# Softmax in a fused gated cross-attention and expert layer: the exponential per group of 64 columns, from PSUM, with its sums

## The chip, the cores and the metric

The kernel runs on one core of one Trainium2 chip. The metric is device time in microseconds (us) of one execution. Engines: PE (TensorE, matmuls), DVE (VectorE), ACT (ScalarE), POOL (GpSimd), SP (issues DMAs). The engines run their own instruction streams in order and wait for one another through semaphores.

## The reference, cut to what matters

1024 tokens (16 sequences of 64) of width 256 go through a layer norm, self attention and cross attention with quantised projections, a gated residual, and a mixture of 16 experts with top-2 routing. The part that the change touches is the softmax of both attentions:

```python
def _gqa(q, k, v):
    scale = 1.0 / np.sqrt(q.shape[-1])
    scores = jnp.einsum('bsghd,btgd->bghst', q, k) * scale
    p = jax.nn.softmax(scores, axis=-1)
    return jnp.einsum('bghst,btgd->bsghd', p, v)
# 8 groups g, 2 heads h per group, head width 128, 64 queries s and 64 keys t for each sequence b
...
core = _gqa(q, k, v).reshape(b, s, nh * d)
...
xout = _gqa(qx, kx, vx).reshape(b, s, nh * d)
```

## The kernel before

The tokens are cut into 8 tiles of 128 (two sequences each). A tile t takes one pass of four steps c = 0 to 3; step number n = 4t + c. Steps c = 0, 1 are self attention, c = 2, 3 cross attention, each for half of the heads. In one step PE makes four projections of 512 columns (`project`, i = 0 to 3: keys, two banks of queries, values), and the work is a pipeline over steps: step n projects for n, transposes the normalised heads of n-1, computes and normalises the scores of n-2, transposes the probabilities and multiplies by the values for n-3, and projects the output of n-4. Tile 0 also carries the preparation of the weights ("folds"). Behind the 8 tiles comes the expert part, which the change does not touch.

The order on each engine is written out by hand in its function `step`; the passes t = 1 to 6 are a hardware loop, the others unrolled. In a step ACT does, in this order: `evacuate` 0 (L647, PSUM to SBUF), `prob_copy` (L692), `norm_bank0` (L668, four 128x128 scalings), `evacuate` 1, the exponential `expo` (L687), `evacuate` 2, `heads_out` 0 (L682), `values_out` (L655), `heads_out` 1 and 2, and `roots` (L659 logarithm, L661 exponential: the inverse square root of the head variance). POOL does the softmax division `normalise` (L535), then `variance` (L509, L511), `coefficients` (L517 to L523, from ACT's root to `cw`), then `norm_bank` 1 and 2 (L529); in step c = 2 also the rounding of the next tile's inputs (L501, L503). ACT's `norm_bank0` waits for `cw` (`coef_done`). DVE does `stats` 0 (L1243), `softmax_in` (L1251 maximum, L1254 subtraction), `stats` 1, `softmax_sum` (L1260, L1263), `stats` 2, and the scaling and quantisation of the attention output (L1270, L1203 to L1214).

The scores of a step stand in one PSUM bank, `score_ps`: 128 partitions (2 heads x 64 queries) by 8 groups of 64 keys. PE uses the same bank for `head_transposes` i = 1 and then for the next scores. PE's order in a step: projection 0, probability transposes, scores, projection 1, values, output, projection 2, head transposes 0, projection 3, head transposes 1 and 2. `ge(engine, semaphore, count)` is a wait that is left out where the count is not positive. `prob` and `probT`, `probn` and the like are parts of `reg1` and `reg2`, which the profile calls `reg`; `raw` is part of `rot`.

Of the kernel before, what the change touches and what calls it, by code (L numbers as in the profile page):

```python
# [24 lines left out]
F32 = mybir.dt.float32  # L25
# [4 lines left out]
ALU = mybir.AluOpType  # L30
ACT = mybir.ActivationFunctionType
AX = mybir.AxisListType
# [76 lines left out]
def build(nc, x, cols, rowc, ident, cen, tri, slot, ctxT, wkvN, wqN, wkN, wvN, wqxN, wpT, rwT, wffn, out):  # L109
    ctx = ExitStack()  # L110
    with ctx:
# [77 lines left out]
        mx = sb("mx", [P, 8], F32)  # L189
        sm = sb("sm", [P, 8], F32)  # L190
        rinv = sb("rinv", [P, 2, 8], F32)
# [152 lines left out]
        max_done = sem("max_done")  # L344
        sub_done = sem("sub_done")
        exp_done = sem("exp_done")
        sum_done = sem("sum_done")
        rinv_done = sem("rinv_done")
# [248 lines left out]
        def _(act):  # L597
# [87 lines left out]
            def expo(w, s):  # L685
                act.wait_ge(sub_done, w + 1)
                act.activation(prob[s], prob[s], ACT.Exp, scale=SCORE_SCALE).then_inc(exp_done, 1)  # L687

# [114 lines left out]
        def _(pe):  # L803
# [61 lines left out]
            def head_transposes(n, c, i):  # L865
                pe.wait_ge((norm0_done, norm1_done, norm2_done)[i], n + 1)
                if i == 1:
                    ge(pe, sub_done, n)
                else:
                    ge(pe, headT_evac, 3 * n + (0, 0, 1)[i])  # L870
# [10 lines left out]
            def scores(w, s):  # L881

                pe.wait_ge(headT_evac, 3 * w + 3)
                ge(pe, sub_done, w)
                for g in range(4):
                    for b in range(2):
                        mm = pe.matmul(score_ps[:, (2 * g + b) * S:(2 * g + b + 1) * S], qT[:, s, 2 * g + b, :],  # L887
                                       kT[:, s, g, b * S:(b + 1) * S], start=True, stop=True)
                mm.then_inc(score_done, 1)
# [229 lines left out]
        def _(ve):  # L1119
# [128 lines left out]
            def softmax_in(w, s):  # L1248
# [3 lines left out]
                ve.wait_ge(max_done, w + 1)  # L1252
                ge(ve, probn_done, w - 1)
                ve.tensor_tensor(prob[s].rearrange("p (g t) -> p g t", t=S), s3,  # L1254
                                 mx[:, :].unsqueeze(2).to_broadcast([P, 8, S]),
                                 ALU.subtract).then_inc(sub_done, 1)

            def softmax_sum(w, s):
                ve.wait_ge(exp_done, w + 1)
                ve.tensor_reduce(sm[:, :], prob[s].rearrange("p (g t) -> p g t", t=S), AX.X,  # L1260
                                 ALU.add).then_inc(sum_done, 1)
                ve.wait_ge(sum_done, w + 1)
                ve.reciprocal(rinv[:, s, :], sm[:, :]).then_inc(rinv_done, 1)  # L1263

# [280 lines left out]
```

## Time and profile before

| | |
|---|---|
| three runs | 478.61, 479.4, 489.06 us; median 479.4 |
| profiled execution | 479.9 us, of which the span from first to last instruction is 478.1 |
| PE busy | 416.2 us (87%) |
| DVE busy | 371.3 us (78%) |
| ACT busy | 281.3 us (59%) |
| POOL busy | 277.4 us (58%) |
| granted TensorE clock, mean | 0.96 of full |

The busy shares are means over a preparation, eight passes and the expert part, which have different limits. A row of the profile names line, engine, operation and tiles (out<-in); "idle" in a row is how long the engine stood still just before the instruction, and the name behind the arrow is what ended that wait.

### The profile page before, as it was taken

What the parts mean: (1) busy time and instruction counts of PE and PEld (TensorE: products, weight loads), DVE (VectorE), ACT (ScalarE), POOL (GpSimd) and SP (SyncE); (2) the same over time, 40 slices, a digit from 0 to 9 for tenths busy, and PEclk for the clock granted to TensorE, in tenths of its full rate; (3) what the DMA queues carried; (4) which work ended last, traced back from release to release, by engine and by line L of the source; (5) the groups of instructions that cost most, each with busy time, mean ns of one, the idle gap of its engine ahead of it and who ended that gap; (6) DMA issues with size and microseconds to landing.
All of it is one profiled execution on the core that took longest, in us unless ns stands there. A gap on an engine that the chain in (4) does not pass through costs nothing.

```text
span 478.1 us, 9942 instructions
## 1 busy us (share of the span) xinstructions
PE 416.2 (87%) x2982; PEld 312.6 (65%) x2982; DVE 371.3 (78%) x832; ACT 281.3 (59%) x610; POOL 277.4 (58%) x401
## 2 busy tenths in 40 slices
PE   0488899999999999999999999999897697999910
PEld 0446567767767776776776777677785585888710
DVE  5987798999999998899899999999679561323236
ACT  3689867767677767867776767777640322333310
POOL 2056496596686867669658677665420660366660
PEclk9989999999999999999999999999888799999975
DMA  8946719999600000000000000000680223244207
GB/s 211 272 156 79 99 60 313 287 318 276 174 0 0 0 0 0 0 0 0 0 0 0 0 0 0 0 3 2 247 346 1 77 101 99 83 123 130 91 19 254
DMA packets 34810, 45.66 MB, mean 95 GB/s; under 512 B 3034, under 2 KB 32223, under 8 KB 33888
## 3 DMA queue, kind: packets, MB, share of 16 engines
q1 hardware_dynamic: 26656, 35.61, 24.0%
q0 software_dynamic: 6992, 9.46, 9.0%
q10 hardware_dynamic: 1136, 0.27, 0.3%
q8 instruction: 13, 0.21, 0.2%
q14 instruction: 13, 0.11, 0.1%
HBM read 28.34 MB, written 24.32 MB: 110 GB/s over the span
## 4 chain that ended last, share of the span: by engine, by line
PE 42%; DVE 18%; POOL 15%; issue 11%; ACT 7%; DMA 5%; SPq 1%; POOLq 1%; ACTq 0%; DVEq 0%
PE proj_ps L860 9%; PE score_ps L887 7%; PE proj_ps L1017 6%; PE pv_ps L909 4%; PE out_ps L919 3%; POOL zbuf L570 3%; POOL xin L501 3%; POOL rot L529 3%; DVE st L1243 3%; DVE yv L1270 2%; ACT rot L647 2%; PE probT_ps L895 2%; PE headT_ps L878 2%; POOL reg L535 2%; ACT qT L682 2%
## 5 line engine op out<-in xcount | busy, mean ns | idle before, releaser
L860 PE MATMUL proj_ps<-arena 128*128 128x512 f16 x384 | 99.7, 382 | 3.9 <-POOL arena L503 3.9
L1243 DVE BATCH_NORM_STATS2 st<-rot 128x6 f32<-128x256 f32 x192 | 72.7, 420 | 13.9 <-ACT rot L647 12.8
L529 POOL TENSOR_TENSOR rot<-rot,cw 128x512 f32<-128x512 f32 x64 | 67.3, 1072 | 2.5
L647 ACT ACTIVATE rot<-proj_ps 128x512 f32<-128x512 f32 x96 | 56.4, 588 | 20.3 <-PE proj_ps L860 18.5
L535 POOL TENSOR_TENSOR reg<-reg,rinv 128x512 f32<-128x512 f32 x32 | 34.6, 1083 | 52.8 <-DVE rinv L1263 52.8
L887 PE MATMUL score_ps<-kT,qT 128*128 128x64 f32 x512 | 62.0, 275 | 0.6 <-ACT qT L682 0.5
L887 PEld LDWEIGHTS score_ps<-kT,qT 128*128 128x128 f32 x512 | 60.3, 193 | 2.4 <-ACT qT L682 2.2
L668 ACT ACTIVATE rot<-rot,cw 128x128 f32<-128x128 f32 x128 | 40.9, 390 | 30.2 <-POOL cw L523 30.2
L860 PEld LDWEIGHTS proj_ps<-arena 128*128 (+1 forms) x384 | 37.4, 103 | 29.6 <-issue 6.2
L852 PE MATMUL proj_ps<-arena 128*128 128x512 f16 x192 | 46.7, 379 | 0.0
L1435 DVE TENSOR_TENSOR arena<-proj_ps,arena 128x256 f32<-128x256 f32 x24 | 10.1, 422 | 46.4 <-ACT arena L754 46.4
L589 POOL DMA_INDIRECT ybuf<-arena,bslot x32 | 31.5, 983 | 24.7 <-DVE arena L1447 19.1
L1270 DVE TENSOR_TENSOR yv<-pv_ps,smi 128x512 bf16<-128x512 f32 x64 | 40.6, 675 | 1.8 <-PE pv_ps L909 1.8
L909 PEld LDWEIGHTS pv_ps<-reg,vv 64*128 64x128 f32 x512 | 31.9, 191 | 13.3 <-issue 11.9
L878 PE MATMUL headT_ps<-idf,rot 128*128 128x128 f32 x256 | 38.6, 273 | 0.4 <-ACT kT L682 0.4
L909 PE MATMUL pv_ps<-reg,vv 64*128 64x128 f32 x512 | 38.1, 289 | 0.7 <-ACT reg L692 0.7
L919 PE MATMUL out_ps<-wp_sb,reg 128*128 128x256 bf16 x256 | 34.3, 278 | 2.3 <-DVE reg L1214 2.3
L687 ACT ACTIVATE reg<-reg 128x512 f32<-128x512 f32 x32 | 20.1, 628 | 25.3 <-DVE reg L1254 25.3
L517 POOL TENSOR_TENSOR nw<-vw,r 128x12 f32<-128x12 f32 x32 | 10.2, 318 | 42.5 <-ACT r L661 42.5
L878 PEld LDWEIGHTS headT_ps<-idf,rot 128*128 128x128 f32 x256 | 30.4, 141 | 6.6 <-issue 0.8
L1017 PE MATMUL proj_ps<-arena 128*128 x128 | 31.5, 390 | 1.1 <-ACT arena L766 0.8
L852 PEld LDWEIGHTS proj_ps<-arena 128*128 (+1 forms) x192 | 18.8, 98 | 15.5
(223 smaller groups left out, 866.1 us busy)
## 6 DMA issues: line engine op xcount, KB each, us to landing
zbuf<-fill SPq DMA_DIRECT2D x1, 16576.5 KB, 60.7
arena<-in_wffn SPq DMA_DIRECT2D x4, 1536.0 KB, 13.7
arena<-zbuf SPq DMA_DIRECT2D x32, 128.5 KB, 2.1
wkv_stage<-in_wkvN SPq DMA_DIRECT2D x1, 2048.0 KB, 15.1
wp_sb<-in_wpT POOLq DMA_DIRECT2D x1, 2048.0 KB, 15.6
wp_sb<-ybuf SPq DMA_DIRECT2D x8, 256.0 KB, 4.5
xs<-in_x SPq DMA_DIRECT2D x2, 512.0 KB, 5.4
vv<-in_wqN POOLq DMA_DIRECT2D x1, 1024.0 KB, 12.6
```

Of the source, the lines that this page charges most:

```text
L529: gp.tensor_tensor(r, r, cw[:, 4 * i:4 * i + 4].unsqueeze(2).to_broadcast([P, 4, D]), ALU.mult)\
L535: gp.tensor_tensor(probn[s].rearrange("p (g t) -> p g t", t=S), prob[s].rearrange("p (g t) -> p g t", t=S), rinv[:, s, :].unsqueeze(2).to_ ...
L647: act.activation(raw[c % 2][i], proj_ps[i % 2][:, :], ACT.Copy).then_inc(proj_evac, 1)
L852: mm = pe.matmul(ps, lhs, w[:, ch, o:o + 512], start=(k == 0), stop=(k == 5))
L860: mm = pe.matmul(ps, lhs, w[kind][:, ch, 512 * b:512 * b + 512], start=(k == 0), stop=(k == 3))
L878: mm = pe.transpose(dst, raw[c % 2][i][:, h * D:(h + 1) * D], idf[:, :])
L887: mm = pe.matmul(score_ps[:, (2 * g + b) * S:(2 * g + b + 1) * S], qT[:, s, 2 * g + b, :], kT[:, s, g, b * S:(b + 1) * S], start=True, sto ...
L909: mm = pe.matmul(pv_ps[b][:, g * P:(g + 1) * P], vv[rows, u, g * D:(g + 1) * D], pT[rows, g * P:(g + 1) * P], start=True, stop=True)
L919: mm = pe.matmul(out_ps[:, 0:H], catq[u % 2][:, h * P:(h + 1) * P], wp[:, 8 * u + h, :], start=(u == 0 and h == 0), stop=(u == NU - 1 and ...
L1017: mm = pe.matmul(up_ps[u % 2][:, b * 2 * P:(b + 1) * 2 * P], z(b, c), wall[:, bass.ds(base[b] + c * 2 * P, 2 * P)] if u >= NSHU else wall[ ...
L1243: ins = ve.bn_stats(st[:, 4 * i + h:4 * i + h + 2, :].rearrange("p h s -> p (h s)"), raw[c % 2][i][:, h * D:(h + 2) * D].rearrange("p (h d ...
L1270: ins = ve.tensor_tensor(y3[:, :, b * S:(b + 1) * S], pv_ps[b][:, :].rearrange("p (h t) -> p h t", t=S), smi[:, 8 * u:8 * u + 8].unsqueeze ...
```

## The change

Before, DVE took the maximum of each group of 64 scores (128x8), subtracted it from the bank while moving it from PSUM to SBUF, ACT took one exponential over 128x512 in place, DVE summed each group and took reciprocals. Now DVE takes the maximum and multiplies it by minus the score scale (`nmx`, 128x8), and ACT reads the scores from PSUM in eight instructions of 128x64, each with its own column of `nmx` as bias; the accumulator output of each gives one column of the sums `sm`. DVE only takes the reciprocals. `sm` and `nmx` have two buffers. PE may use `score_ps` again when the exponential is done (`exp_done`) instead of the subtraction (`sub_done`).

```diff
--- before.py
+++ after.py
@@ -187,7 +187,8 @@
         xm = sb("xm", [P, XW], F16)
 
         mx = sb("mx", [P, 8], F32)
-        sm = sb("sm", [P, 8], F32)
+        sm = sb("sm", [P, 2, 8], F32)
+        nmx = sb("nmx", [P, 2, 8], F32)
         rinv = sb("rinv", [P, 2, 8], F32)
         NLH = 12
         st = sb("st", [P, NLH, 3], F32)
@@ -342,9 +343,8 @@
         headT_evac = sem("headT_evac")
         score_done = sem("score_done")
         max_done = sem("max_done")
-        sub_done = sem("sub_done")
+        neg_done = sem("neg_done")
         exp_done = sem("exp_done")
-        sum_done = sem("sum_done")
         rinv_done = sem("rinv_done")
         probn_done = sem("probn_done")
         prob_out = sem("prob_out")
@@ -683,8 +683,13 @@
                                scale=col(kind + "w"), bias=col(kind + "b")).then_inc(headT_evac, 1)
 
             def expo(w, s):
-                act.wait_ge(sub_done, w + 1)
-                act.activation(prob[s], prob[s], ACT.Exp, scale=SCORE_SCALE).then_inc(exp_done, 1)
+                act.wait_ge(neg_done, w + 1)
+                ge(act, probn_done, w - 1)
+                ge(act, rinv_done, w - 1)
+                for g in range(8):
+                    ins = act.activation(prob[s][:, g * S:(g + 1) * S], score_ps[:, g * S:(g + 1) * S], ACT.Exp,
+                                         bias=nmx[:, s, g:g + 1], scale=SCORE_SCALE, accum_out=sm[:, s, g:g + 1])
+                ins.then_inc(exp_done, 1)
 
             def prob_copy(w, s):
                 act.wait_ge(probT_done, w + 1)
@@ -865,7 +870,7 @@
             def head_transposes(n, c, i):
                 pe.wait_ge((norm0_done, norm1_done, norm2_done)[i], n + 1)
                 if i == 1:
-                    ge(pe, sub_done, n)
+                    ge(pe, exp_done, n)
                 else:
                     ge(pe, headT_evac, 3 * n + (0, 0, 1)[i])
                 ps = (headT_ps, score_ps, headT_ps)[i]
@@ -881,7 +886,7 @@
             def scores(w, s):
 
                 pe.wait_ge(headT_evac, 3 * w + 3)
-                ge(pe, sub_done, w)
+                ge(pe, exp_done, w)
                 for g in range(4):
                     for b in range(2):
                         mm = pe.matmul(score_ps[:, (2 * g + b) * S:(2 * g + b + 1) * S], qT[:, s, 2 * g + b, :],
@@ -1250,17 +1255,13 @@
                 ve.wait_ge(score_done, w + 1)
                 ve.tensor_reduce(mx[:, :], s3, AX.X, ALU.max).then_inc(max_done, 1)
                 ve.wait_ge(max_done, w + 1)
-                ge(ve, probn_done, w - 1)
-                ve.tensor_tensor(prob[s].rearrange("p (g t) -> p g t", t=S), s3,
-                                 mx[:, :].unsqueeze(2).to_broadcast([P, 8, S]),
-                                 ALU.subtract).then_inc(sub_done, 1)
+                ge(ve, exp_done, w - 1)
+                ve.tensor_scalar(nmx[:, s, :], mx[:, :], -SCORE_SCALE, None, ALU.mult).then_inc(neg_done, 1)
 
             def softmax_sum(w, s):
                 ve.wait_ge(exp_done, w + 1)
-                ve.tensor_reduce(sm[:, :], prob[s].rearrange("p (g t) -> p g t", t=S), AX.X,
-                                 ALU.add).then_inc(sum_done, 1)
-                ve.wait_ge(sum_done, w + 1)
-                ve.reciprocal(rinv[:, s, :], sm[:, :]).then_inc(rinv_done, 1)
+                ge(ve, probn_done, w - 1)
+                ve.reciprocal(rinv[:, s, :], sm[:, s, :]).then_inc(rinv_done, 1)
 
             def over_smooth(w, u):
 
```

ACT, inside the looped passes, step c = 0, before: from the scaling of head bank 0 to the value bank.

```order
L668 ACTIVATE rot<-rot,cw 128x128 [waits coef_done]
L668 ACTIVATE rot<-rot,cw 128x128 x3
L647 ACTIVATE rot<-proj_ps 128x512 [waits headT_done,proj_done]
L687 ACTIVATE reg<-reg 128x512 [waits sub_done]
L647 ACTIVATE rot<-proj_ps 128x512 [waits headT_done,proj_done]
L682 ACTIVATE kT<-headT_ps,colv 128x512 [waits score_done,headT_done]
L655 ACTIVATE vv<-proj_ps,colv 128x512 [waits pv_done,proj_done]
```

And the same place now.

```order
L668 ACTIVATE rot<-rot,cw 128x128 [waits coef_done]
L668 ACTIVATE rot<-rot,cw 128x128 x3
L647 ACTIVATE rot<-proj_ps 128x512 [waits headT_done,proj_done]
L690 ACTIVATE reg,sm<-score_ps,nmx 128x64 [waits rinv_done,probn_done,neg_done]
L690 ACTIVATE reg,sm<-score_ps,nmx 128x64 x7
L647 ACTIVATE rot<-proj_ps 128x512 [waits headT_done,proj_done]
L682 ACTIVATE kT<-headT_ps,colv 128x512 [waits score_done,headT_done]
```

Eight instructions stand where one stood, between `evacuate` 1 and `evacuate` 2; nothing else on ACT moved.

DVE, the softmax of one step, before.

```order
L1251 TENSOR_REDUCE mx<-score_ps 128x8 [waits score_done]
L1254 TENSOR_TENSOR reg<-score_ps,mx 128x512 [waits probn_done,max_done]
L1243 BN_STATS st<-rot 128x6 [waits proj_evac]
L1243 BN_STATS st<-rot 128x6
L1260 TENSOR_REDUCE sm<-reg 128x8 [waits exp_done]
L1263 RECIPROCAL rinv<-sm 128x8 [waits sum_done]
```

And now.

```order
L1256 TENSOR_REDUCE mx<-score_ps 128x8 [waits score_done]
L1259 TENSOR_SCALAR nmx<-mx 128x8 [waits exp_done,max_done]
L1248 BN_STATS st<-rot 128x6 [waits proj_evac]
L1248 BN_STATS st<-rot 128x6
L1264 RECIPROCAL rinv<-sm 128x8 [waits probn_done,exp_done]
```

The two passes over 128x512 are gone; one operation on 128x8 came in.

## Rows read from the trace of the kernel before

**Rows 1.** The page: busy time by engine, and the chain that ended last by engine.
```profile
PE 416.2 (87%) x2982; PEld 312.6 (65%) x2982; DVE 371.3 (78%) x832; ACT 281.3 (59%) x610; POOL 277.4 (58%) x401
PE 42%; DVE 18%; POOL 15%; issue 11%; ACT 7%; DMA 5%; SPq 1%; POOLq 1%; ACTq 0%; DVEq 0%
```

**Rows 2.** Windows: start:end, length, busy of each engine, then TensorE clock, DMA share, GB/s.
```profile
core 0: us, PE busy (x) PEld busy (x) DVE busy (x) ACT busy (x) POOL busy (x), PEclk, DMA share, GB/s
50.00:66.00 16.00, 13.93 (x100) 9.10 (x98) 12.82 (x26) 13.66 (x27) 9.52 (x12) 1.00 0.34 46
84.00:345.00 261.00, 254.45 (x1951) 186.24 (x1950) 240.18 (x493) 186.09 (x407) 180.19 (x257) 0.99 0.20 57
```

**Rows 3.** Timeline of TensorE (start, length, idle before in brackets): first projection of two passes.
```profile
260.68 1.03 PE L860 MATMUL proj_ps<-arena 128*128 128x512 f16 x4 [0.55 <-POOL arena L503]
...
299.80 1.02 PE L860 MATMUL proj_ps<-arena 128*128 128x512 f16 x4 [0.56 <-POOL arena L503]
```

**Rows 4.** Groups by line and form (busy us, mean ns), the softmax instructions.
```profile
L1254 DVE TENSOR_TENSOR reg<-score_ps,mx 128x512 f32<-128x512 f32 x32 | 22.1, 691 | 1.6
L1260 DVE TENSOR_REDUCE sm<-reg 128x8 f32<-128x512 f32 x32 | 21.8, 682 | 1.9 <-ACT reg L687 1.4
L687 ACT ACTIVATE reg<-reg 128x512 f32<-128x512 f32 x32 | 20.1, 628 | 25.3 <-DVE reg L1254 25.3
L1263 DVE RECIPROCAL rinv<-sm 128x8 f32<-128x8 f32 x32 | 6.5, 203 | 1.1
```

**Rows 5.** Timeline of ACT, and two rows of POOL, through one step (c = 0).
```profile
264.60 1.28 ACT L668 ACTIVATE rot<-rot,cw 128x128 f32<-128x128 f32 x4 [0.64 <-POOL cw L523]
265.79 0.57 ACT L647 ACTIVATE rot<-proj_ps 128x512 f32<-128x512 f32 x1
267.17 0.63 ACT L687 ACTIVATE reg<-reg 128x512 f32<-128x512 f32 x1 [0.81 <-DVE reg L1254]
268.15 0.60 ACT L647 ACTIVATE rot<-proj_ps 128x512 f32<-128x512 f32 x1 [0.35 <-PE proj_ps L860]
...
271.61 0.21 ACT L661 ACTIVATE r<-vl 128x12 f32<-128x12 f32 x1
271.75 0.60 ACT L647 ACTIVATE rot<-proj_ps 128x512 f32<-128x512 f32 x1
...
271.97 0.22 POOL L517 TENSOR_TENSOR nw<-vw,r 128x12 f32<-128x12 f32 x1 [1.54 <-ACT r L661]
...
273.81 0.21 POOL L523 TENSOR_TENSOR cw<-nw,r 128x12 f32<-128x12 f32 x1
...
274.06 1.28 ACT L668 ACTIVATE rot<-rot,cw 128x128 f32<-128x128 f32 x4 [1.22 <-POOL cw L523]
```

**Rows 6.** Timeline of ACT: exponentials of the three other steps, what follows them, start of the pass.
```profile
262.11 0.21 ACT L659 ACTIVATE vl<-va 128x12 f32<-128x12 f32 x1 [0.88 <-POOL va L509]
...
275.72 0.62 ACT L687 ACTIVATE reg<-reg 128x512 f32<-128x512 f32 x1
277.37 0.60 ACT L647 ACTIVATE rot<-proj_ps 128x512 f32<-128x512 f32 x1 [1.03 <-PE proj_ps L860]
...
286.79 0.63 ACT L687 ACTIVATE reg<-reg 128x512 f32<-128x512 f32 x1 [1.80 <-DVE reg L1254]
287.33 0.58 ACT L647 ACTIVATE rot<-proj_ps 128x512 f32<-128x512 f32 x1
...
294.36 0.57 ACT L647 ACTIVATE rot<-proj_ps 128x512 f32<-128x512 f32 x1
...
296.67 0.60 ACT L647 ACTIVATE rot<-proj_ps 128x512 f32<-128x512 f32 x1 [0.95 <-PE proj_ps L860]
...
298.40 0.60 ACT L655 ACTIVATE vv<-proj_ps 128x512 f32<-128x512 f32 x1 [0.47 <-PE proj_ps L852]
```

**Rows 7.** Timeline of DVE: the maximum in the steps c = 0, 2 and 3.
```profile
265.65 0.67 DVE L1251 TENSOR_REDUCE mx<-score_ps 128x8 f32<-128x512 f32 x1
...
285.37 0.66 DVE L1251 TENSOR_REDUCE mx<-score_ps 128x8 f32<-128x512 f32 x1
...
293.66 0.67 DVE L1251 TENSOR_REDUCE mx<-score_ps 128x8 f32<-128x512 f32 x1
```

**Rows 8.** Groups by line and form: the ACT instructions nearest to the new ones.
```profile
L655 ACT ACTIVATE vv<-proj_ps,colv 128x512 f32<-128x512 f32 x16 | 11.0, 687 | 0.6 <-PE proj_ps L860 0.2
L661 ACT ACTIVATE r<-vl 128x12 f32<-128x12 f32 x32 | 6.8, 213 | 1.0
L668 ACT ACTIVATE rot<-rot,cw 128x128 f32<-128x128 f32 x128 | 40.9, 390 | 30.2 <-POOL cw L523 30.2
```

## The prediction

> **What bounds the kernel now.** I read the page first, for shares. PE is busy 87% of the span and carries 42% of the chain that ended last; DVE is busy 78%, ACT only 59% [rows 1]. That invites the conclusion that work may go from DVE to ACT for nothing. The windows view then shows the stage where the softmax lives: from 84 to 345 us, PE is busy 254.45 of 261.00 us, DVE 240.18, ACT 186.09, at a granted clock of 0.99 [rows 2]. All that any change of DVE or ACT can win there is PE's idle time, 261.00 - 254.45 = 6.55 us. Last I read the timeline of one pass. It takes 299.80 - 260.68 = 39.12 us, 9.78 per step [rows 3].
>
> ACT's mean hides a loop that is nearly as long as a step. ACT scales head bank 0 at 264.60, evacuates, takes the exponential at 267.17, evacuates again, runs on to its roots, which POOL waits for (271.97), and POOL's coefficients, ready at 273.81 + 0.21, let ACT scale bank 0 of the next step at 274.06 [rows 5]. That is 9.46 us, in a steady state in which every step closes the loop once. Its slack around the exponential is small: in this step 0.81 us before it and 0.35 behind it [rows 5]. Whatever the exponential takes beyond that lengthens the step, unless there is slack further on in the loop. So the question is not ACT's total of 59% but how long eight small instructions take in this place.
>
> **What goes.** On DVE the subtraction, 691 ns, and the sum, 682 ns, 32 times each [rows 4]; 1.37 us per step. In comes one operation on 128x8, which I cost as its nearest row, the reciprocal at 203 ns [rows 4]. DVE loses 1.17 us of work per step, 37 us in all. I count nothing for it beyond the earlier start of the exponential: PE and the loop above set the step. DVE also gets a new wait: its reciprocal now waits directly for the exponential, with `stats` 2 and the output quantisation queued behind. The work gone (1.17 us) and DVE's idle time (20.8 us in 261) [rows 2] cover it in the main case, since the quantised output is used a step later. DVE's moved waits for old buffers (`probn_done`, `exp_done` of two steps back) are past long before and cost nothing. No DMA is moved.
>
> **What comes on ACT: the price X of eight exponentials.** The trace has no 64-column ACTIVATE and no accumulator output. Length of one: exponentials of 12 columns take 213 ns and of 512 take 628 ns [rows 8, 4], so 0.83 ns per column. The nearest form, read from PSUM with a column operand, is L655 at 687 ns for 512 columns [rows 8]; 448 columns fewer gives 687 - 372 = 315 ns. One starts before the last ends: four scalings of mean 390 ns take 1.28 us together, (1.28 - 0.39) / 3 = 0.30 us apart [rows 5, 8], so 0.09 to 0.10 us overlap. Low end: 0.215 us apart and the accumulator free, X = 7 x 0.215 + 0.315 = 1.82 us. High end: each is followed, without overlap, by a second instruction as long as the 12-column one (213 ns), X = 8 x 0.528 = 4.22 us. Between them, by the rows: overlap lost and the read free is 0.315 apart; overlap kept and a read that takes what the 12-column exponential takes before the next instruction starts (271.75 - 271.61 = 0.14) [rows 5] is 0.355. I take 0.34, X = 2.7 us, against 0.63 now.
>
> The Trainium skill (ScalarE: Activation LUTs, What ACT_TABLE_LOAD costs) has an estimate of its own: 280 ns and 0.83 per column with a column as bias, 93 ns of overlap, and no charge for the accumulator; that would be 8 x 240 + 93 ns = 2.0 us for the eight, and by the sums below some 491 us in place of 508. Against the change speaks a statement on the other engine (VectorE: DVE Perf Modes, Two Vector instructions with no wait between them), that an accumulator output makes two instructions of one; no run here shows either yet.
>
> **What of X lies on the path**, per pass, from each step's rows. c = 0: the maximum ends at 265.65 + 0.67 = 266.32 [rows 7]; with 0.03 of hand-over, 0.20 for the negation and 0.05 to ACT the exponential starts at 266.60, and the next instruction can start 0.10 before it ends, 266.50 + X, against 268.15 now: later by X - 1.65. c = 1: the exponential started at 275.72 with no wait, so it cannot start earlier; the evacuation behind it started at 277.37 [rows 6]: X - 1.75. c = 2: the maximum ends at 286.03 [rows 7], the exponential starts at 286.31 instead of 286.79, the evacuation stood at 287.33 [rows 6]: X - 1.12. c = 3: the maximum ends at 294.33 [rows 7], ACT is free at about 294.84 (0.10 before the end of the evacuation at 294.36) [rows 6]; the next one stood at 296.67: X - 1.93, and behind it are two more slacks, 0.47 before the values and 0.88 before the logarithm at the start of the pass [rows 6], so X - 3.28, nothing below that. The sum is 3X - 4.52 + max(0, X - 3.28); at X = 2.7, 3.58 us per pass, 0.9 per step.
>
> Seven passes (t = 1 to 7) give 25.1 us. The two exponentials of t = 0 fall among the folds, where ACT is busy 13.66 of 16 us [rows 2]; I price them like the loop's, 1.8 us. The two in the drain run beside the router's first work; the last of them lies near the path, and there X + 0.2 replaces 0.69 + 0.63 + 0.68 [rows 4]: 0.9 us. **Sum 27.8 us.** On the profiled 479.9 us that is 507.7; the median of the runs is 479.4, half a microsecond lower, which changes nothing. Forecast 508 us.
>
> PE gets the same delay through its own waits: head transposes 1 now wait for the exponential's end, and head transposes 2 for ACT's `heads_out` 0. That is where its stall will stand; it is the same 0.9 us per step, not another.
>
> **The rivals.** A change within 2% (9.6 us) cannot be told from none here; slower means above 489.0.
>
> - *The eight fit into the idle time.* ACT has 4.0 us idle around the exponentials of steps 0, 1 and 2 alone (0.81 + 0.35, 1.03, 1.80) [rows 5, 6]. If X is at most 1.5 us, 190 ns apiece, the sum is zero or below, and what DVE gives up may return a part of PE's 6.55 us: 474 to 481 us, not slower. For it speaks ACT's 59%; against it, that even the overlapped pitch from the rows is 215 ns. 5%.
> - *The accumulator is free*, X from 1.8 to 2.3: at 1.82 the sum is 0.94 x 7 + 0.5 = 7 us, 487; at 2.3 it is 2.38 x 7 + 1.7 = 18, 498. The 2% bound lies at X = 1.93. The skill's 2.0 us stands here. 17%.
> - *The forecast*, X from 2.3 to 3.2: at 3.2, 5.08 x 7 + 2.5 + 1.4 = 39.5, so 498 to 519. 56%.
> - *ACT becomes the bound*: the read is a second instruction that does not overlap. From X = 3.3 all four steps stretch, and at 4.2 ACT's 186.09 / 261.00 x 9.78 = 7.0 us per step become 10.6. The sum at 4.22 is 9.08 x 7 + 4.5 + 2.4 = 70.5: 519 to 550. For it speaks that nothing in the trace excludes it. 17%.
> - *The clock falls as well.* PE's busy share in the passes would drop from 97% to near 90%. In 50 to 66 us it was 87% busy and the clock still 1.00 [rows 2], which speaks against. A clock of 0.93 would add up to 0.7 us to a PE step of 9.5, at most 20 us: 528. 5%.
>
> **How the numbers follow.** 508 is the likeliest case. The range of 490 to 537 leaves out the first rival, the lower part of the second and the upper half of the fourth, about 18%. Slower by over 2%: all cases but the first and a third of the second, some 0.88; within 2%: 0.10; faster needs 9.6 us where PE has 6.55 to give: 0.02.
>
> **What would show it.** Right: L690 about 0.34 us apart, ACT near 350 us busy in all, PE's busy share in the passes down to about 90% with waits at head transposes 1 and 2 for ACT, passes of 42 to 43 us, DVE idle before L1264, and no change behind the last pass. Wrong price: another pitch of L690; then the sum above, with the measured X, should give the time. Wrong mechanism: X near 2.7 and passes still near 39 us, which would say that the loop through the roots had slack I did not see, or passes much above 43, which would say that DVE's new wait or POOL's order adds its own.

## The result, and the profile after

**510.86 us** (median of four runs, 509.78 to 512.83) against 479.87 before (median of four, 478.61 to 489.06): 1.0687 times the time, 95% interval 1.0656 to 1.0717. Slower by 31 us. Some executions come out longer than the others of the same kernel (489.06 here, and one of 1090.52 among the four of the version fill below), and the ratios are of the rest. The profiled execution took 510.67 us, with a span of 508.8, against 479.9 and 478.1 before; the spans differ by 30.7.

The page, busy time by engine and the chain by engine, answers to [rows 1].
```profile
PE 427.8 (84%) x2982; PEld 314.1 (62%) x2982; DVE 336.1 (66%) x800; ACT 335.7 (66%) x1090; POOL 280.0 (55%) x401
ACT 31%; PE 27%; DVE 19%; issue 9%; POOL 7%; DMA 4%; ACTq 1%; SPq 1%; POOLq 1%; DVEq 0%
```
ACT's share of the chain went from 7% to 31%, though ACT is busy only 66% of the span. DVE has lost 35 us of work, and the kernel is slower: neither busy share says what bounds it.

The groups by line and form (busy us, mean ns, idle before and its releaser) answer to [rows 4].
```profile
L690 ACT ACTIVATE reg<-score_ps,nmx 128x64 f32<-128x64 f32 x256 | 76.1, 323 | 20.3 <-DVE nmx L1259 20.3
L690 ACT ACTIVATION_READ_ACCUMULATOR reg<-score_ps,nmx 128x1 f32 x256 | 55.2, 216 | 0.0
L883 PE MATMUL headT_ps<-idf,rot 128*128 128x128 f32 x256 | 39.7, 278 | 11.7 <-ACT kT L682 11.7
L883 PE MATMUL score_ps<-idf,rot 128*128 128x128 f32 x128 | 19.8, 277 | 10.1 <-ACT reg L690 10.1
L1259 DVE TENSOR_SCALAR nmx<-mx 128x8 f32<-128x8 f32 x32 | 7.5, 235 | 1.6
L1264 DVE RECIPROCAL rinv<-sm 128x8 f32<-128x8 f32 x32 | 6.5, 203 | 57.6 <-ACT reg L690 57.6
```
Three things to see. Each exponential brings an `ACTIVATION_READ_ACCUMULATOR`, an instruction of its own that reads out the sum: 256 of them stand beside 256 exponentials. PE waits 10.1 us at head transposes 1 for the exponential and 11.7 at head transposes 2 for `kT`. DVE waits 57.6 us at the reciprocal, where it waited for ACT's exponential 1.4 us before [rows 4].

The windows of the stage answer to [rows 2]; the second row is the stretch between the last head transposes of tile 0's pass and those of the last pass (65.14 to 338.27 before).
```profile
84.00:345.00 261.00, 241.26 (x1803) 169.61 (x1802) 194.12 (x429) 212.21 (x740) 170.81 (x237) 0.99 0.21 51
66.88:364.86 297.98, 275.68 (x2070) 194.36 (x2069) 222.13 (x494) 242.55 (x845) 192.57 (x272) 0.99 0.23 57
```
PE is busy 92.4% of the same 261 us, where it was 97.5%, at the same granted clock of 0.99. The clock of the passes has no part in it.

The timeline of PE at the same places as [rows 3], with the two waits of step c = 0 between them.
```profile
278.92 1.03 PE L865 MATMUL proj_ps<-arena 128*128 128x512 f16 x4 [0.53 <-POOL arena L503]
...
287.93 0.63 PE L883 MATMUL score_ps<-idf,rot 128*128 128x128 f32 x4 [0.54 <-ACT reg L690]
289.00 0.66 PE L883 MATMUL headT_ps<-idf,rot 128*128 128x128 f32 x4 [0.44 <-ACT kT L682]
...
321.32 1.02 PE L865 MATMUL proj_ps<-arena 128*128 128x512 f16 x4 [0.53 <-POOL arena L503]
```
A pass takes 321.32 - 278.92 = 42.40 us, against 39.12: 3.28 more.

The timeline of ACT, from the exponential of c = 0 to that of c = 1, answers to [rows 5].
```profile
285.31 0.32 ACT L690 ACTIVATE reg<-score_ps,nmx 128x64 f32<-128x64 f32 x1 [0.72 <-DVE nmx L1259]
285.52 0.19 ACT L690 ACTIVATION_READ_ACCUMULATOR reg<-score_ps,nmx 128x1 f32 x1
285.61 0.31 ACT L690 ACTIVATE reg<-score_ps,nmx 128x64 f32<-128x64 f32 x1
...
287.35 0.34 ACT L690 ACTIVATE reg<-score_ps,nmx 128x64 f32<-128x64 f32 x1
287.55 0.24 ACT L690 ACTIVATION_READ_ACCUMULATOR reg<-score_ps,nmx 128x1 f32 x1
287.64 0.63 ACT L647 ACTIVATE rot<-proj_ps 128x512 f32<-128x512 f32 x1
288.12 0.83 ACT L682 ACTIVATE kT<-headT_ps,colv 128x512 f32<-128x512 f32 x1
...
293.58 1.28 ACT L668 ACTIVATE rot<-rot,cw 128x128 f32<-128x128 f32 x4 [1.36 <-POOL cw L523]
294.77 0.57 ACT L647 ACTIVATE rot<-proj_ps 128x512 f32<-128x512 f32 x1
295.25 0.30 ACT L690 ACTIVATE reg<-score_ps,nmx 128x64 f32<-128x64 f32 x1
```
The pairs stand 0.29 us apart. From the first start to the last end it is 287.79 - 285.31 = 2.48 us, **the measured X**, and the next instruction starts 2.33 after the first. At c = 1 the exponentials follow `evacuate` 1 with no wait: before them ACT waited 1.36 us for `cw`, POOL's coefficients. In the steps c = 0 and c = 2 they wait for DVE instead, for the negated maximum (0.72 here, 1.28 at 306.51). What DVE did before 306.51 is the other half of the profile:
```profile
297.74 0.20 DVE L1264 RECIPROCAL rinv<-sm 128x8 f32<-128x8 f32 x1 [1.60 <-ACT reg L690]
298.23 0.76 DVE L1248 BATCH_NORM_STATS2 st<-rot 128x6 f32<-128x256 f32 x2 [0.29 <-ACT rot L647]
298.91 1.27 DVE L1271 TENSOR_TENSOR yv<-pv_ps,smi 128x512 bf16<-128x512 f32 x2
...
303.86 1.14 DVE L1229 TENSOR_SCALAR xm<-xm 128x1024 f16<-128x1024 bf16 x1
304.93 0.75 DVE L1248 BATCH_NORM_STATS2 st<-rot 128x6 f32<-128x256 f32 x2
305.60 0.67 DVE L1256 TENSOR_REDUCE mx<-score_ps 128x8 f32<-128x512 f32 x1
306.31 0.17 DVE L1259 TENSOR_SCALAR nmx<-mx 128x8 f32<-128x8 f32 x1
```
DVE waits for the exponentials of c = 1, then 0.29 us for `evacuate` 2, which stands behind them on ACT. From 298.23 on it is never idle: it works off everything it has queued behind the reciprocal and releases the exponentials of c = 2. That is a second loop, of 306.51 - 295.25 = 11.26 us, and it contains X as the first one does. Below, the **root loop** is the prediction's (bank 0 scaled, exponentials, roots, POOL's coefficients, next bank 0), and the **DVE loop** is this one (exponentials, reciprocal, DVE's queue, maximum and negation, next exponentials).

**Where the 30.7 us stand.** The last head transposes of tile 0's pass come 1.7 later (66.88 against 65.14), passes 1 to 6 take 3.30 more each (19.8), the last pass 5.1 more; the last head transposes so come 26.6 later (364.86 against 338.27). Most of the rest is the clock. The chain of waits of before, its last rows ahead of the expert part:
```profile
351.46 1.73 PE score_ps L887 x16
353.19 3.56 PE headT_ps L947 x24
356.75 2.03 PE pv_ps L909 x16
358.81 1.30 DVE yv L1270 x2
```
The same of after:
```profile
378.31 3.31 PE score_ps L892 x16
381.61 5.04 PE headT_ps L952 x24
386.65 2.03 PE pv_ps L914 x16
388.71 1.30 DVE yv L1271 x2
```
From the last head transposes to the last scores it is 13.19 us before and 13.45 after. From there to DVE's `yv` the same matmuls take 358.81 - 351.46 = 7.35 us before and 10.40 after: 3.05 us more. The windows of these stretches, before:
```profile
351.46:358.80 7.34, 7.34 (x57) 7.08 (x57) 4.63 (x9) 1.43 (x4) 1.04 (x1) 0.72 0.64 273
```
and after:
```profile
364.86:378.31 13.45, 9.42 (x80) 8.24 (x78) 9.43 (x18) 11.48 (x36) 6.81 (x10) 0.94 0.95 384
378.31:388.70 10.39, 10.39 (x57) 10.13 (x57) 2.31 (x5) 3.08 (x17) 1.04 (x1) 0.50 0.44 186
```
The granted clock (third number from the end) was 0.72 of full speed before and 0.50 after, which is 1.2 of 2.4 GHz throughout. Length times clock is the same, 7.34 x 0.72 = 5.3 and 10.39 x 0.50 = 5.2: the same work, and only the clock differs. In the stretch ahead PE had been busy 9.42 of 13.45 us after, and 10.14 of 13.19 before; why the clock was low for longer is not shown. All behind that, the expert part, adds 0.8. So 1.7 + 19.8 + 5.1 + 0.3 + 3.0 + 0.8 = 30.7.

### The profile page after: what moved, and what is told of

Its sections match the earlier page's. It is cut to its first block, busy times and chain, and to the rows that moved or that the text cites. A ratio compares the mean times of both kernels' runs of the same rounds, so it can differ in the third digit from the quotient of the medians.

```text
span 508.8 us, 10456 instructions
## 1 busy us (share of the span) xinstructions
PE 427.8 (84%) x2982; PEld 314.1 (62%) x2982; DVE 336.1 (66%) x800; ACT 335.7 (66%) x1090; POOL 280.0 (55%) x401
## 4 chain that ended last, share of the span: by engine, by line
ACT 31%; PE 27%; DVE 19%; issue 9%; POOL 7%; DMA 4%; ACTq 1%; SPq 1%; POOLq 1%; DVEq 0%
ACT reg L690 12%; ACT rot L647 5%; PE proj_ps L1022 4%; PE score_ps L892 4%; PE proj_ps L865 4%; ACT qT L682 4%; ACT rot L668 3%; DVE st L1248 2%; DVE yv L1271 2%; ACT kT L682 2%; ACT vv L655 2%; POOL zbuf L570 2%; PE headT_ps L883 2%; PE proj_ps L857 2%; DVE yv L1208 2%
## 5 line engine op out<-in xcount | busy, mean ns | idle before, releaser
L865 PE MATMUL proj_ps<-arena 128*128 128x512 f16 x384 | 101.3, 387 | 3.2 <-POOL arena L503 3.2
L690 ACT ACTIVATE reg<-score_ps,nmx 128x64 f32<-128x64 f32 x256 | 76.1, 323 | 20.3 <-DVE nmx L1259 20.3
L535 POOL TENSOR_TENSOR reg<-reg,rinv 128x512 f32<-128x512 f32 x32 | 33.4, 1044 | 73.2 <-DVE rinv L1264 73.2
L647 ACT ACTIVATE rot<-proj_ps 128x512 f32<-128x512 f32 x96 | 57.7, 601 | 4.8 <-PE proj_ps L865 3.1
L865 PEld LDWEIGHTS proj_ps<-arena 128*128 (+1 forms) x384 | 37.7, 104 | 29.4 <-issue 6.4
L690 ACT ACTIVATION_READ_ACCUMULATOR reg<-score_ps,nmx 128x1 f32 x256 | 55.2, 216 | 0.0
L883 PE MATMUL headT_ps<-idf,rot 128*128 128x128 f32 x256 | 39.7, 278 | 11.7 <-ACT kT L682 11.7
L857 PE MATMUL proj_ps<-arena 128*128 128x512 f16 x192 | 46.7, 379 | 0.0
L589 POOL DMA_INDIRECT ybuf<-arena,bslot x32 | 31.5, 983 | 25.2 <-DVE arena L1448 19.5
L1264 DVE RECIPROCAL rinv<-sm 128x8 f32<-128x8 f32 x32 | 6.5, 203 | 57.6 <-ACT reg L690 57.6
L1271 DVE TENSOR_TENSOR yv<-pv_ps,smi 128x512 bf16<-128x512 f32 x64 | 40.7, 677 | 3.4 <-PE pv_ps L914 3.4
L1436 DVE TENSOR_TENSOR arena<-proj_ps,arena 128x256 f32<-128x256 f32 x24 | 10.1, 423 | 46.1 <-ACT arena L759 46.1
L517 POOL TENSOR_TENSOR nw<-vw,r 128x12 f32<-128x12 f32 x32 | 11.1, 346 | 47.8 <-ACT r L661 47.8
## 6 DMA issues: line engine op xcount, KB each, us to landing
wp_sb<-ybuf SPq DMA_DIRECT2D x8, 256.0 KB, 5.0
```

Of the source, the lines that this page charges most:

```text
L647: act.activation(raw[c % 2][i], proj_ps[i % 2][:, :], ACT.Copy).then_inc(proj_evac, 1)
L690: ins = act.activation(prob[s][:, g * S:(g + 1) * S], score_ps[:, g * S:(g + 1) * S], ACT.Exp, bias=nmx[:, s, g:g + 1], scale=SCORE_SCALE, ...
L857: mm = pe.matmul(ps, lhs, w[:, ch, o:o + 512], start=(k == 0), stop=(k == 5))
L865: mm = pe.matmul(ps, lhs, w[kind][:, ch, 512 * b:512 * b + 512], start=(k == 0), stop=(k == 3))
L883: mm = pe.transpose(dst, raw[c % 2][i][:, h * D:(h + 1) * D], idf[:, :])
L1271: ins = ve.tensor_tensor(y3[:, :, b * S:(b + 1) * S], pv_ps[b][:, :].rearrange("p (h t) -> p h t", t=S), smi[:, 8 * u:8 * u + 8].unsqueeze ...
```

## The experiments

Every ratio is to the kernel before, run beside it on the same chip. That took 484.99 us beside the first four versions, 483.96 beside dead, fill, pad and noacc_fill, and 479.37 beside the last two, so compare ratios rather than times. "After" is the changed kernel. The pass is read from two starts of POOL's L478 or L501 one pass apart.

### The price of the sums: noacc

```diff
- ACT.Exp, bias=nmx[:, s, g:g + 1], scale=SCORE_SCALE, accum_out=sm[:, s, g:g + 1])
+ ACT.Exp, bias=nmx[:, s, g:g + 1], scale=SCORE_SCALE)
...
+ ve.tensor_reduce(sm[:, s, :], prob[s].rearrange("p (g t) -> p g t", t=S), AX.X, ALU.add).then_inc(sum_done, 1)
+ ve.wait_ge(sum_done, w + 1)
```

> The changed kernel without the accumulator: the eight exponentials with their biases stay, DVE sums the groups again (128x512 to 128x8) before the reciprocal. Theory (the length X of the eight on ACT sets the loss): without the accumulator reads the eight start 0.20 to 0.22 us apart, X = 1.7 to 1.8 us instead of 2.48, and the loss shrinks by more than half: 487 to 493 us. Rival (eight separate instructions with a column as bias cost it, the accumulator is nearly free or hidden): X stays near 2.4 and the time near 505 to 512, or higher since DVE has its sum back.

**505.04 us, ratio 1.0402 (1.0300 to 1.0504)**, pass 41.8 us. The timeline of ACT, the exponentials of one step as one row:
```profile
281.68 1.74 ACT L691 ACTIVATE reg<-score_ps,nmx 128x64 f32<-128x64 f32 x8 [0.72 <-DVE nmx L1260]
```
Eight take 1.74 us, 0.20 apart: the accumulator costs 2.48 - 1.74 = 0.74 us per step. The price of the sum came out as expected and the time did not: with X 0.74 shorter the prediction's formula gives 3 x 1.74 - 4.52 = 0.70 us per pass, and 2.7 were measured. This is where the theory of the single loop first failed. The group of the exponential says where to look next:
```profile
L691 ACT ACTIVATE reg<-score_ps,nmx 128x64 f32<-128x64 f32 x256 | 55.8, 330 | 31.5 <-DVE nmx L1260 31.5
```
ACT now waits 31.5 us for DVE's negated maximum, against 20.3 after. DVE got its sum back behind the exponential, 0.69 us, so that the DVE loop is hardly shorter. And the negation itself, an operation on 128x8, grew from a mean of 235 ns to 535. POOL and DVE at c = 1:
```profile
289.30 2.04 POOL L530 TENSOR_TENSOR rot<-rot,cw 128x512 f32<-128x512 f32 x2
290.45 0.91 DVE L1260 TENSOR_SCALAR nmx<-mx 128x8 f32<-128x8 f32 x1
```
In 15 of the 32 steps no POOL operation runs beside the negation, and it takes 0.17 us; in the other 17 it takes 0.34 to 0.92. Here it ends 0.02 us behind POOL's pair. So in noacc the exponentials wait for DVE in all four steps of a pass, 0.39 us at c = 1 and c = 3, where after they don't wait.

### One exponential for all groups: onemax

The sum is DVE's again, as in noacc.

```diff
- for g in range(8):
-     ins = act.activation(prob[s][:, g * S:(g + 1) * S], ..., bias=nmx[:, s, g:g + 1], scale=SCORE_SCALE, accum_out=...)
+ act.activation(prob[s], score_ps[:, :], ACT.Exp, bias=nmx[:, s, :], scale=SCORE_SCALE).then_inc(exp_done, 1)
...
- ve.tensor_reduce(mx[:, :], s3, AX.X, ALU.max).then_inc(max_done, 1)
+ ve.tensor_reduce(mx[:, :], score_ps[:, :], AX.X, ALU.max).then_inc(max_done, 1)
```

> One exponential of 128x512 straight from PSUM with one bias column, the negated maximum over all 512 scores of a row instead of one per group; sums by DVE as in the kernel before; no subtraction pass. X is then about 0.69 us (from the 687 ns of the like-shaped scaling). Theory (PE sets the step, DVE's freed 0.5 us per step are worth next to nothing): 475 to 481 us, no change that can be told from the kernel before. Rival (DVE's time is worth something since its queue delays the maximum in two of four steps): 465 to 472 us.

**481.05 us, ratio 0.9938 (0.9895 to 0.9980)**, median of 12 executions, pass 38.85. One maximum per row serves all eight groups, so a single ACTIVATE with a bias column does it:
```profile
L690 ACT ACTIVATE reg<-score_ps,nmx 128x512 f32<-128x512 f32 x32 | 21.7, 679 | 15.5 <-DVE nmx L1257 15.5
```
679 ns in place of 628: the subtraction from DVE is taken in for 0.05 us. The loss of the change comes with cutting the exponential in eight and with the sums, not with taking it from PSUM or with a bias. This is the only version faster than before, by 0.6%. PE is busy 256.0 of the same 261 us here, so the 0.5 us per step taken off DVE has little left to win.

### More of the same: twelve

```diff
+ for g in range(4):
+     act.activation(pad[:, g, :], score_ps[:, g * S:(g + 1) * S], ACT.Exp,
+                    bias=nmx[:, s, g:g + 1], scale=SCORE_SCALE, accum_out=pacc[:, g:g + 1])
```

> The changed kernel with four more exponentials of 64 columns with accumulator before the eight, into a tile that nobody reads: X grows by 4 x 0.29 = 1.16 us to 3.64. Theory (all of X is on the path once the slack is used up, so a pass grows by 3X or 4X): passes grow by 3.5 to 4.6 us, 511 + 25 to 33 = 536 to 544 us. Rival (the loss is a fixed price of the new waits, and not the length of the exponentials): under 520 us.

**555.84 us, ratio 1.1471 (1.1392 to 1.1550).** More than expected, even by ratio (about 550). Passes are uneven, 46.4 to 49.5 us with a mean of 47.4, and the granted clock in them fell to 0.93 to 0.97. Four more pairs, 1.16 us, cost 5.0 us per pass, where all four steps stretched by them would be 4.6. That fits X counting in full in every step once the slack is gone; how much of the 5.0 is the clock is not separated.

### A shorter loop through the roots: short

The first try at taking this loop out of the way: POOL leaves out the Newton step behind the root (L517 to L519 and L511), so `cw` is ready earlier; the root is used as ACT gives it (the constant `newt[:, 1, :]` becomes 1.0 in place of 1.5).
```diff
- chained(nchain, gp.tensor_tensor(nw[:, 0, :], vw[:, :], r0[:, :], ALU.mult), 3 * n + 1)
...
- gp.tensor_tensor(cw[:, :], nw[:, 0, :], r0[:, :], ALU.mult).then_inc(coef_done, 1)
+ gp.tensor_tensor(cw[:, :], r0[:, :], newt[:, 1, :], ALU.mult).then_inc(coef_done, 1)
```

> The changed kernel with POOL's Newton step left out (three small operations on 128x12 and one before them; the head scale is then taken from the plain logarithm and exponential, a little less accurate). ACT's and PE's work is unchanged, only the way from ACT's root to the coefficients is about 1.5 us shorter. Theory of the prediction (the loop scale bank 0, exponential, roots, POOL's coefficients sets the step): the loop shrinks by 1.5 us, and a pass goes back towards the 39.1 us that PE needs: 485 to 492 us. Rival (another loop of about the same length closes through the scores: scores, maximum, exponential, head transposes 1 and 2, their evacuation, next scores): 507 to 511 us, almost no change.

**542.56 us, ratio 1.1222 (1.1146 to 1.1297)**, passes of 46 to 47 us. Both expectations missed, on the side that none had: with less work in the loop it is some 30 us slower than after. The timeline of POOL in one step of this run:
```profile
280.87 2.92 POOL L523 TENSOR_TENSOR rot<-rot,cw 128x512 f32<-128x512 f32 x2
```
and of DVE at the same time, and one step later:
```profile
280.75 0.69 DVE L1209 TENSOR_TENSOR ys<-yv,ym 128x1024 f16<-128x1024 bf16 x1
281.48 1.41 DVE L1213 TENSOR_TENSOR reg<-ys,ym 128x1024 bf16<-128x1024 f16 x1
...
292.91 1.41 DVE L1209 TENSOR_TENSOR ys<-yv,ym 128x1024 f16<-128x1024 bf16 x1
294.35 1.41 DVE L1213 TENSOR_TENSOR reg<-ys,ym 128x1024 bf16<-128x1024 f16 x1
```
POOL's `norm_bank` 1 and 2 took 2.04 us (after, at 293.63) and DVE's two operations 0.69 each. Moved earlier, they fall together: 2.92 and, for DVE's two, 1.41 in place of 0.69 once or twice. DVE's lie in the DVE loop. Over the run DVE is busy 369.8 us against 336.1 after, with the same 800 operations. The Trainium skill (SBUF — State Buffer, Who interferes with whom) has a rule for it: a DVE `tensor_tensor` with both inputs in SBUF contends with a GpSimd instruction that reads SBUF, and the ports that the two share are locked for one of them at a time. The run agrees: 1.41 is about the operation's own 0.69 and a wait for part of one POOL operation of 1.04. For the question asked this run says nothing, since it lengthens one loop while it shortens the other. That DVE's 33.7 us are the loss is read from these rows; no run moved the operations apart, and the granted clock in the passes, 0.93 to 0.96, has a share that is not separated.

### The loop through DVE, made longer: dead

One line more behind the reciprocal:
```diff
+ ve.tensor_reduce(dead[:, :], reg2[:, 1024:1536].rearrange("p (g t) -> p g t", t=S), AX.X, ALU.add)
```

> The changed kernel with one dead sum of 128x512 added on DVE behind the reciprocal of each step (about 0.7 us, into a tile that nobody reads; ACT, PE and POOL unchanged). Theory of the prediction (DVE's work is off the path, only ACT's loop carries the exponential): no change, 508 to 513 us. New theory (a second loop closes through DVE: exponential, reciprocal, statistics, output scaling and quantisation, next maximum, next exponential; it binds in the steps c = 2 and c = 0 and is 0.5 us short of binding in the others): a pass grows by 2 x 0.7 + 2 x 0.2 = 1.8 us, 521 to 526 us.

**523.49 us, ratio 1.0862 (1.0782 to 1.0943)**, passes of 44.4 us. A DVE operation that nobody uses, 634 ns long, beside the 57.6 us that DVE waits for ACT after, comes with passes 2.0 us longer. The time is in the range of the new theory and out of that of the prediction. ACT's wait for DVE grew:
```profile
L691 ACT ACTIVATE reg<-score_ps,nmx 128x64 f32<-128x64 f32 x256 | 76.2, 325 | 30.1 <-DVE nmx L1260 30.1
```
With DVE's idle time as cover it would have been free. It lies behind the wait, and so in the loop: the step from c = 1 to c = 2, where the DVE loop binds, went from 11.26 to 12.19 us. The 2.0 us are not all the loop's. In four of the five passes from 84 us on the granted clock fell to 0.5 for 3.4 us, and ACT waited for PE's projections there (1.44 us at 281.62); they took 44.4 to 45.6. The one pass without such a fall took 43.58 us, 1.2 more than after.

### The loop through DVE, made shorter: fill

The scaling of the attention output (`over_smooth`, L1271) needs nothing of this step's exponentials. It moves from behind `stats` 2 to ahead of the reciprocal, into DVE's wait.
```diff
+ if live(n, 3):
+     over_smooth(n - 3, (c - 3) % NU)
...
- if live(n, 3):
-     over_smooth(n - 3, (c - 3) % NU)
```

> The changed kernel with DVE's order altered: the scaling of the attention output (two 128x512 operations, 1.27 us) stands before the reciprocal instead of behind the third statistics, so DVE does it while it waits for the eight exponentials (it stood idle 1.6 to 2.0 us there). No operation is added or taken away. New theory (the loop through DVE binds in two of four steps): the loop through DVE loses 1.27 us, passes fall from 42.4 to 39.8 to 40.7 us, 486 to 497 us, the rest of the loss is left to the loop through the roots. Theory of the prediction (only ACT's loop): 508 to 512 us.

**496.5 us, ratio 1.0258 (1.0162 to 1.0353)**, pass 39.67 in place of 42.40. Nothing is left out; one piece of work has another place. The time is at the upper end of the new theory's range; the prediction's had 508 to 512. The window of the passes:
```profile
84.00:345.00 261.00, 255.99 (x1949) 183.46 (x1948) 216.25 (x466) 230.09 (x801) 174.13 (x253) 1.00 0.21 52
```
and the reciprocal:
```profile
L1264 DVE RECIPROCAL rinv<-sm 128x8 f32<-128x8 f32 x32 | 6.5, 203 | 21.1 <-ACT reg L690 21.1
```
PE's idle time in the 261 us fell from 19.7 to 5.0, DVE's at the reciprocal from 57.6 to 21.1. With all eight exponentials and their reads in place, the passes are 0.55 us above those of before. So another order on DVE gives back nearly all that the change costs in the passes. By the traces the run is still 17.1 us longer than the kernel before (spans of 495.2 and 478.1): 8.9 are there at the last scores, at 360.2 us against 351.3, and a granted clock of 0.72 in 354 to 378 us is part of what follows. What holds the last 0.55 us per pass is open. ACT waits for `cw` in every step (0.65 to 1.03 us), as it does in the kernel before; and at c = 0, 2 and 3 the exponentials still wait 0.52, 0.39 and 0.25 for the negation, which takes 0.91 and 0.95 us at c = 2 and 3, beside POOL, in place of 0.17 and 0.21.

### The same length without the relief of DVE: pad

```diff
  act.activation(prob[s], prob[s], ACT.Exp, scale=SCORE_SCALE)
+ for j in range(6):
+     ins = act.activation(pad[:, j, :], cenf[:, :], ACT.Copy)
  ins.then_inc(exp_done, 1)
```
This one starts from the kernel before.

> The kernel before, with six copies of 128x128 on ACT behind its single exponential and ahead of the semaphore that DVE's sum waits for, so that the exponential's slot is about as long (2.3 to 2.5 us) as the eight with accumulator, while DVE still subtracts and sums. Theory of the prediction (the length of the slot on ACT is all, DVE's relief is worth nothing): like the changed kernel, 508 to 513 us. New theory (the loop through DVE carries the slot too, and the change took 1.17 us per step out of that loop): without that relief it is about 3.7 us per pass worse than the changed kernel, 530 to 540 us.

**513.53 us, ratio 1.0661 (1.0563 to 1.0759)**, pass 42.8. The copies turned out shorter than meant: six took 1.29 us, so that the slot to the next instruction is 1.73 us (244.81 - 243.08) and not the change's 2.33. The time lies where the theory of the prediction had it, but for a slot 0.6 us shorter than the one it was forecast for, so it does not speak for that theory. What it does tell: 0.6 us less on ACT, with DVE's subtraction and sum kept, gives the same time as the change. DVE's relief of 1.17 us is worth about 0.6 us of ACT per step; the prediction had it at nothing.

### Both loops short: noacc_fill

The edits of noacc and of fill together, as they stand above.

> Eight exponentials with their biases and no accumulator (DVE sums), and DVE's output scaling ahead of the sum, as in the run fill. New theory (two loops, both carry the length X of the eight): with X = 1.74 and the DVE loop 1.27 shorter, PE's own 39.1 us per pass binds almost everywhere, 480 to 487 us. Rival (the loss of the eight without accumulator comes from something else, such as the negated maximum's way to ACT): 495 to 502 us.

**483.54 us, ratio 1.0031 (0.9980 to 1.0082)**, pass 39.00. Eight exponentials per group from PSUM cost nothing that can be measured, once no read stands between them and DVE's wait is filled. Each edit alone left 4.0% and 2.6%. By passes: 42.40 us with neither edit, 41.8 with noacc, 39.67 with fill, 39.00 with both, so the order on DVE gives back 2.7 to 2.8 with the accumulator or without it. PE's new wait for the exponential's end is in this version as in after, so it costs nothing by itself.

### The root loop, made longer: long and before_long

The middle multiplication of POOL's Newton step is done three times, in after and in before.
```diff
- chained(nchain, gp.tensor_tensor(nw[:, 1, :], nw[:, 0, :], r0[:, :], ALU.mult), 3 * n + 2)
+ for k in range(2, 5):
+     chained(nchain, gp.tensor_tensor(nw[:, 1, :], nw[:, 0, :], r0[:, :], ALU.mult), 5 * n + k)
```

> The changed kernel with one of POOL's small coefficient operations (128x12, 0.2 to 0.65 us as traced) done three times instead of once, the same values each time: the way from ACT's root to the coefficients is 0.6 to 1.3 us longer, ACT, PE and DVE have the same work. Two-loop theory (the loop through the roots binds in the steps c = 0 to 1 and 2 to 3, the loop through DVE in the others): a pass grows by 2 x 1.0 us and up to 0.6 more, from 42.4 to 44 to 45, 522 to 531 us. Rival (the root loop isn't on the path, all of the loss is the loop through DVE or PE's waits): 509 to 514 us.

> The kernel before with the same two extra POOL operations per step. Two-loop theory: there the loop through the roots has idle time around the short exponential (0.35 to 1.8 us per step), so most of the extra 0.6 to 1.3 us vanishes: passes of 39.1 to 40, 480 to 488 us. Rival (POOL's chain is on the path of every step in both kernels): the same 12 to 20 us as in the changed kernel, 493 to 500 us.

**long: 516.68 us, ratio 1.0801 (1.0732 to 1.0870)**, pass 43.93, 1.54 above after. **before_long: 483.37, ratio 1.0127 (1.0047 to 1.0207)**, pass 39.54, 0.43 above before. The timeline of POOL in long:
```profile
288.06 1.66 POOL L519 TENSOR_TENSOR nw<-nw,r 128x12 f32<-128x12 f32 x3
289.80 0.21 POOL L520 TENSOR_TENSOR nw<-nw,newt 128x12 f32<-128x12 f32 x1
290.08 0.21 POOL L524 TENSOR_TENSOR cw<-nw,r 128x12 f32<-128x12 f32 x1
```
Three took 1.66 us where one took 0.65, but the addition behind them took 0.21 in place of 0.74. ACT's wait for `cw` at c = 1 grew from 1.36 to 1.93 us: the chain is 0.57 longer, below the 0.6 to 1.3 expected, and the time fell between the two expectations (509 to 514 and 522 to 531). The times from the first exponential of one step to that of the next, in one looped pass each, show where it counts:

| from c to c | 0 to 1 | 1 to 2 | 2 to 3 | 3 to 0 | pass |
|---|---|---|---|---|---|
| before | 8.55 | 11.07 | 8.30 | 11.18 | 39.1 |
| after | 9.94 | 11.26 | 9.85 | 11.35 | 42.4 |
| long | 10.50 | 11.29 | 10.42 | 11.72 | 43.9 |

The 0.57 us stand in full in two of the four steps, 0 to 1 and 2 to 3, where the two-loop theory has the root loop binding. The 0.37 of 3 to 0 are DVE's: the negation at c = 0 took 0.55 us in place of 0.17. If the root loop bound all four steps it would be 4 x 0.57 = 2.3 us per pass, and if it bound none, zero. In before_long ACT's wait for `cw` grew by the same 0.57 us (1.22 to 1.79 at c = 1), and the pass by only 0.43: there the chain has slack.

## Why the prediction held, and where it did not

**The loop over ACT, not ACT's total.** Held. ACT's busy share never came near the limit, and the chain of waits of after runs from the exponentials over `evacuate` 2, `kT`, the roots, POOL's coefficients and back (the ACT timeline above).

**What goes on DVE.** The costs were right: `nmx` 235 ns against 203 assumed, 371.3 - 336.1 = 35.2 us of busy time gone against 37. The sentence "I count nothing for it beyond the earlier start of the exponential", and the one that DVE's new wait is covered by work gone and idle time, are **the step that failed**. They give DVE no part in the steady step. The relief is worth about 0.6 us per step (pad), and the wait is not covered: everything queued behind the reciprocal, 8.2 us in the step shown, has to run between the exponentials of one step and the maximum of the next (dead, fill). Idle time of an engine covers nothing that is queued behind the wait which makes the idle time.

**The price X.** 2.7 forecast, 2.48 measured: pitch 0.29, not 0.34. The bounds (1.82 and 4.22) held it. "Overlap kept and a separate read" was the right case; the read adds 0.29 - 0.20 = 0.09 us to the pitch where 0.14 was assumed, and without it the pitch is 0.20 where 0.215 was the low end. The estimate from the Trainium skill's figures (ScalarE: Activation LUTs, What ACT_TABLE_LOAD costs) was 2.0 us; the traces have 1.74 without the accumulator and 2.48 with it, so it is high on the one and leaves out the other. What the Trainium skill states of VectorE (VectorE: DVE Perf Modes, Two Vector instructions with no wait between them), an accumulator read as a second instruction, is seen here on ScalarE: 256 reads beside 256 exponentials.

**What of X lies on the path.** At X = 2.48 the formula gives 3 x 2.48 - 4.52 = 2.92 us per pass; 3.28 were measured. It is short because at c = 2 and c = 0 the exponentials start when DVE releases them, not when the maximum stood before: in the formula's picture the maximum is a fixed point, in the kernel it moves with the last exponential.

**The sum.** With the measured X it would have been 20.4 + 1.5 + 0.7 = 22.6 us, 502.5 in place of 510.7. The missing 8.1: 2.3 in passes 1 to 6 (6 x 0.38), 2.2 in the last pass, 0.3 before t = 1, and 3.4 behind the last pass, of which 3.05 is the clock. In the forecast the price of X, 0.22 us too high, added 27.8 - 22.6 = 5.2 us and stood against these 8.1: 27.8 forecast, 30.7 measured. So the number is partly luck, two errors that cancel. The last pass, 5.1 in place of 2.9, has no run of its own. In both kernels DVE has work of this pass alone ahead of the maximum at c = 0 and c = 2 (L1339 and L1341, L1135 to L1352 after), and in after the exponentials wait 1.84 and 1.92 us for it where the passes before have 0.72 and 1.28: the DVE loop again. The granted clock was also 0.5 for 3.4 us in that pass. How much each of them costs stays open.

**Signs foretold.** PE's waits for ACT at head transposes 1 and 2: there, 10.1 and 11.7 us. Passes of 42 to 43: 42.40. PE near 90%: 92.4. DVE idle before L1264: 57.6 us. ACT near 350 us busy: 335.7, as the pitch was smaller. No change behind the last pass: the expert part 0.8, but 3.05 in PE's last matmuls ahead of it.

**The rivals.** "The eight fit" and "the accumulator is free" are out by X = 2.48. What the second would have given is not shown: noacc has its X, but also the sum back on DVE. "ACT becomes the bound" needed reads that don't overlap; they overlap. "The clock falls as well" did not happen in the passes (0.99), in the drain it did.

## What to carry to other kernels

Before work is moved between two engines that hand results back and forth, write down every closed loop of waits that goes through the moved piece, with all that is queued in order behind each wait, and not only the loop that binds now: here two loops share the exponential, each binds in two of the four steps, and the forecast had only one. Where an engine shows idle time at a wait, look for work that doesn't depend on it and put it ahead of the wait; that one edit gave back 2.7 of the 3.3 us per pass. Many small instructions cost their pitch times their number on an engine that is in a loop: the same exponential in one piece cost 0.68 us and in eight 1.74, or 2.48 with sums. And before an experiment is read, look at the lengths of operations that the edit did not touch: moving work on DVE or POOL changes which operations of the two meet, and here that added up to 0.7 us to one of 128x8.

## What was not expected of the hardware

- **Accumulator reads cost less than they last.** Each takes 0.19 to 0.24 us and starts 0.20 behind its exponential, yet adds only 0.09 us to the pitch.
- **Lengths grow down the row.** Exponentials go from 0.30 to 0.34 us and reads from 0.19 to 0.24 within the eight, while their starts stay 0.29 apart. Instructions behind them stay longer too, `kT` 0.83 at 288.12 against 0.77 before, until ACT is idle once. Starts barely move by it: `kT` starts 0.48 us behind the evacuation ahead of it, against 0.50 before. In noacc the mean of an exponential is 330 ns though eight of them take 1.74 us, so a mean length here says nothing of what one costs.
- **Less work on POOL slowed DVE.** In short, DVE's `tensor_tensor` from SBUF went from 0.69 to 1.41 us and POOL's pair from 2.04 to 2.92 when they met.
- **POOL's small operations are long where DVE's quantisation runs.** Of after's 192 operations on 128x12, the 87 that overlap in time with one of DVE's two `tensor_tensor` L1215 and L1219 take 558 ns on average, the other 105 take 244. So three in a row took 1.66 us in long and the next one 0.21, and an edit of such a chain doesn't add its own mean. It is the collision of short again, seen from POOL, and that of the negation in noacc is its like.
